# A four-layer graph network on one core: digraph mixes in float16 halves, delta turned by a transfer, norm statistics on ScalarE, the turned adjacency read from memory

## The reference, cut to what matters

```
x = layernorm(layer(x) + x)      # mean and variance over the 384 features, eps 1e-5
```

```
u = h @ h.T / sqrt(D); a = softmax(u); delta = a * adj
attn = delta / (sum(delta, -1) + 1e-10)
ctx = (attn * upper) @ (h @ wl.T + bl) + diag(attn) * (h @ ws.T + bs) + (attn * lower) @ (h @ wr.T + br)
h = relu((ctx - mean) / sqrt(var + 1e-12) * g + beta)
```

## Time and profile before

| | |
|---|---|
| median of 3 runs | 2745.75 us (2744.03 to 2746.03) |
| the profiled execution's own time | 2747.06 us |
| its span, first to last instruction | 2745.3 us |
| TensorE busy | 2590.6 us, 94% (granted clock 0.985 in the mean) |
| VectorE busy | 2315.3 us, 84% |
| GpSimd busy | 2123.3 us, 77% |
| ScalarE busy | 1758.2 us, 64% |

### The profile page before, as it was taken

The page is one execution under the profiler, slowest core; times in us unless marked ns, Lnnn a source line. Parts: engine busy times, 40 slices in busy tenths (PEclk is TensorE's granted clock), DMA queues, the critical chain, the costliest instruction groups (busy, mean ns, idle before and its releaser), DMA issues.

```text
span 2745.3 us, 90305 instructions
## 1 busy us (share of the span) xinstructions
PE 2590.6 (94%) x33792; PEld 1932.8 (70%) x33792; DVE 2315.3 (84%) x8232; ACT 1758.2 (64%) x4628; POOL 2123.3 (77%) x3211
## 2 busy tenths in 40 slices
PE   5899889999999999999999999999999999989996
PEld 4677667767677777777777777777776777667764
DVE  6789887879888888888888888888888888888877
ACT  6646666556666666666666666666666565666546
POOL 6577868777788788888788888888887777777675
PEclk9899999999999999999999999999999999999997
DMA  7733454344444544544545454454554453354315
GB/s 175 157 71 79 81 94 81 74 77 78 89 84 76 95 81 84 94 88 78 89 87 91 83 96 82 80 93 88 88 81 75 82 93 70 77 90 95 60 37 107
DMA packets 800731, 238.95 MB, mean 87 GB/s; under 512 B 767664, under 2 KB 799536, under 8 KB 800304
## 3 DMA queue, kind: packets, MB, share of 16 engines
q1 hardware_dynamic: 791840, 218.23, 44.8%
q10 hardware_dynamic: 8464, 14.94, 1.8%
HBM read 31.72 MB, written 12.58 MB: 16 GB/s over the span
## 4 chain that ended last, share of the span: by engine, by line
PE 54%; DVE 19%; POOL 11%; issue 5%; DMA 5%; ACT 4%; SPq 2%; DVEq 0%; POOLq 0%; ACTq 0%
PE bank L848 7%; PE bank L849 7%; PE bank L850 7%; PE bank L839 6%; PE bank L840 6%; PE bank L841 6%; DMA region<-region 3%; DVE region L1024 3%; PE bank L935 2%; PE bank L878 2%; PE bank L928 2%; PE bank L936 2%; POOL region L644 2%; POOL ab L671 2%; PE bank L864 1%
## 5 line engine op out<-in xcount | busy, mean ns | idle before, releaser
L839 PE MATMUL bank<-region,w_hi 128*128 128x128 f16 x3960 | 687.7, 220 | 7.4 <-DMA region<-region 2.6
L840 PE MATMUL bank<-region,w_hi 128*128 128x128 f16 x3960 | 686.6, 220 | 0.0
L841 PE MATMUL bank<-region,w_lo 128*128 128x128 f16 x3960 | 686.6, 220 | 0.0
L848 PE MATMUL bank<-w_hi,region 128*128 128x384 f16 x1815 | 596.5, 329 | 30.2 <-DMA region<-region 20.7
L849 PE MATMUL bank<-w_lo,region 128*128 128x384 f16 x1815 | 595.6, 328 | 0.0
L850 PE MATMUL bank<-w_hi,region 128*128 128x384 f16 x1815 | 595.6, 328 | 0.0
L655 POOL TENSOR_TENSOR region<-region 128x512 f16<-128x512 f32 x330 | 383.9, 1164 | 185.9 <-ACT region L776 184.1
L770 ACT ACTIVATE region<-region,small 128x128 f32<-128x128 f32 x1320 | 419.5, 392 | 79.3 <-DVE small L1030 61.1
L839 PEld LDWEIGHTS bank<-region,w_hi 128*128 128x128 f16 x3960 | 389.0, 98 | 32.5 <-issue 7.7
L840 PEld LDWEIGHTS bank<-region,w_hi 128*128 128x128 f16 x3960 | 388.8, 98 | 12.3 <-issue 5.8
L841 PEld LDWEIGHTS bank<-region,w_lo 128*128 128x128 f16 x3960 | 388.8, 98 | 0.0
(11 more groups left out here) (217 smaller groups left out, 7742.0 us busy)
## 6 DMA issues: line engine op xcount, KB each, us to landing
region<-region SPq DMA_TRANSPOSE x715, 3.1
last_unit<-w_dram ACTq DMA_DIRECT2D x19, 576.0 KB, 6.1
x<-x_dram SPq DMA_DIRECT2D x55, 192.0 KB, 2.6
out_dram<-region SPq DMA_DIRECT2D x55, 192.0 KB, 2.1
adj<-adj_dram SPq DMA_DIRECT2D x55, 64.0 KB, 2.3
rows<-rows_dram ACTq DMA_DIRECT2D x5, 576.0 KB, 4.4
last_unit<-last_unit SPq DMA_TRANSPOSE x117, 3.1
last_unit<-x_dram SPq DMA_DIRECT2D x9, 192.0 KB, 2.5
```

The lines of the kernel that those rows point to most:

```text
L839: pe.matmul(dst, lhsT=w_hi[:, w, k, cols], rhs=t_hi[u][:, k, :], start=(k == 0), stop=False)
L840: pe.matmul(dst, lhsT=w_hi[:, w, k, cols], rhs=t_lo[u][:, k, :], start=False, stop=False)
L841: last = pe.matmul(dst, lhsT=w_lo[:, w, k, cols], rhs=t_hi[u][:, k, :], start=False, stop=(k == DT - 1))
L848: pe.matmul(dst, lhsT=t_hi[u][:, k, :], rhs=w_hi[:, w, k, :], start=(k == 0), stop=False)
```

## The change

The mixes of the digraph layer become float16 products. `delta` is divided by its row sum and split into high and low (ScalarE, then VectorE), both turned by one transfer (128 x 256 float16), and masked by float16 triangles of 512 columns. Left and right product get their bias on VectorE, into the stage tile `z`, then a high part (ScalarE) and a low part (GpSimd); the right one's bias waits until the left one's low part has been read out of `z`. The self product keeps its way. The mix is six float16 products. The transposed adjacency is an input of its own and is loaded into `mask` by SP after the masked scores of layer 0. For the six norms over 384 features with a residual or in the digraph layer, the sum comes from the accumulator of the addition, and ScalarE makes the mean and the sum of squared distances. `PARTS`, `PERIOD` (22.0233) and `SHIFTED` (now one number per batch and stage for batches 0 to 15 and 50 to 63; before, one per batch for 0 to 11 and 50 to 63) are new; `plan()` is otherwise the same.

Core of the diff (declarations, signals, the tables of the planner and renamed constants are left out):

```diff
             def load_adj(i, k):
+                sp.wait_ge(*topped.at(i, HG - 1, DT - 1))
+                sp.dma_start(adj_t[i % UNITS], adj_t_d[i]).then_inc(adj_t_landed.of(i), 16)
...
+            def delta_turn(i, layer):
+                u = i % UNITS
+                sp.wait_ge(*mixed_out.at(i, "low delta", layer))
+                sp.dma_start_transpose(delta_t[u], delta_hl[u].rearrange("p a n -> p (a n)")).then_inc(landed.of(i), 16)
...
             def denominator(i, layer):
...
-                pool.tensor_scalar(col(u, EPS), col(u, DENOM), col(u, DENOM), 1e-12, ALU.mult, ALU.mult).then_inc(gpsimd_done.of(i), 1)
+                pool.tensor_tensor(col(u, INVERSE), col(u, DENOM), constant(MINUS_ONE), ALU.pow).then_inc(gpsimd_done.of(i), 1)
...
             def residual(i, layer):
-                pool.wait_ge(*numbers.at(i, "residual mv", layer))
-                pool.tensor_tensor(col(u, VAR), mv[u][:, 1:2], constant(LN_EPS), ALU.add).then_inc(gpsimd_done.of(i), 1)
+                pool.wait_ge(*scalar_done.at(i, "spread", layer))
+                pool.tensor_scalar(col(u, VAR), col(u, SQUARES), 1.0 / D, 1e-5, ALU.mult, ALU.add).then_inc(gpsimd_done.of(i), 1)
...
-                pool.tensor_scalar(col(u, SHIFT), mv[u][:, 0:1], col(u, ROOT), -1.0, ALU.mult, ALU.mult)\
-                    .then_inc(gpsimd_done.of(i), 1)
+                pool.tensor_tensor(col(u, SHIFT), col(u, MINUS_MEAN), col(u, ROOT), ALU.mult).then_inc(gpsimd_done.of(i), 1)
...
-            def turn_adj(i, k):
-                act.wait_ge(*multiplied.at(i, "adj"))
-                act.activation(adj_t[i % UNITS], bank("turn_adj", k, i)[:, 0:N], ACT.Copy).then_inc(scalar_done.of(i), 1)
...
+            def high_delta(i, layer):
+                act.wait_ge(*gpsimd_done.at(i, "row scale", layer))
+                act.activation(delta_hl[u][:, 0, :], delta[u], ACT.Copy, scale=col(u, INVERSE)).then_inc(scalar_done.of(i), 1)
+
+            def spread(i, layer):
+                act.wait_ge(*mixed_out.at(i, "added", layer))
+                act.activation(col(u, MINUS_MEAN), col(u, SUM), ACT.Copy, scale=-1.0 / D).then_inc(scalar_done.of(i), 1)
+                act.wait_ge(*scalar_done.at(i, "minus mean", layer))
+                act.activation(score_at[u], z[u], ACT.Square, bias=col(u, MINUS_MEAN), accum_out=col(u, SQUARES))\
+                   .then_inc(scalar_done.of(i), 1)
...
-                pe.transpose(bank("turn_delta", layer, i)[:, 0:N], delta[u], ident).then_inc(multiplied.of(i), 1)
...
             def mix(i, k):
-                    for w in L2_W[k - 2]:
-                        pe.wait_ge(*biased.at(i, "made", w))
+                    for w in (left, right):
+                        pe.wait_ge(*low_of_shifted.at(i, "made", w))
                     pe.wait_ge(*mixed_out.at(i, "delta3", k - 2))
-                    pe.matmul(made[:, 0:D], lhsT=triangles[u][:, 0, :], rhs=proj[u][0], start=True, stop=False)
-                    pe.matmul(made[:, 0:D], lhsT=triangles[u][:, 1, :], rhs=proj[u][2], start=False, stop=True)\
-                      .then_inc(multiplied.of(i), 1)
+                    for side, w in enumerate((left, right)):
+                        high, low = (triangles[u][:, side, n, :] for n in range(2))
+                        h = side_of(u, w)
+                        pe.matmul(dst, lhsT=high, rhs=h[:, 0, :], start=(side == 0), stop=False)
+                        pe.matmul(dst, lhsT=high, rhs=h[:, 1, :], start=False, stop=False)
+                        last = pe.matmul(dst, lhsT=low, rhs=h[:, 0, :], start=False, stop=(side == 1))
+                    last.then_inc(multiplied.of(i), 1)
...
             def add_bias(i, w):
+                    if w in SIDES[1::2]:
+                        dve.wait_ge(*low_of_shifted.at(i, "made", w - 2))
+                    scale, dst, src, bias = 1.0 / WSCALE, shifted[w][u], made[:, 0:D], rows[:, ROW_OF[w], :]
...
+            def delta_low(i, layer):
+                dve.wait_ge(*scalar_done.at(i, "high delta", layer))
+                dve.scalar_tensor_tensor(delta_hl[u][:, 1, :], delta[u], col(u, INVERSE), delta_hl[u][:, 0, :], ALU.mult, ALU.subtract)\
+                   .then_inc(mixed_out.of(i), 1)
...
             def turn_delta(i, layer):
-                dve.wait_ge(*multiplied.at(i, "delta", layer))
-                dve.tensor_tensor_reduce(out=score[u][:, 2, :], in0=turned, in1=ident, scale=1.0, scalar=0.0, op0=ALU.mult,
+                dve.tensor_tensor_reduce(out=score[u][:, 0, :], in0=delta[u], in1=ident, scale=col(u, INVERSE), scalar=0.0, op0=ALU.mult,
                                          op1=ALU.add, accum_out=col(u, DIAGONAL)).then_inc(numbers.of(i), 1)
-                dve.tensor_tensor(triangles[u], turned.unsqueeze(1).broadcast_to([128, 2, N]), tri[:, 0:2, :], ALU.mult)\
-                   .then_inc(mixed_out.of(i), 1)
+                dve.wait_ge(*landed.at(i, "delta", layer))
+                dve.wait_ge(*numbers.at(i, "diagonal", layer))
+                dve.tensor_tensor(triangles[u], delta_t[u].unsqueeze(1).broadcast_to([128, 2, 2, N]),
+                                  tri[:, :, :].unsqueeze(2).broadcast_to([128, 2, 2, N]), ALU.mult).then_inc(mixed_out.of(i), 1)
...
             def inner(i, k):
-                    dve.scalar_tensor_tensor(made[:, 0:D], proj[u][1], col(u, DIAGONAL), made[:, 0:D], ALU.mult, ALU.add)\
-                       .then_inc(numbers.of(i), 1)
-                    dve.wait_ge(*numbers.at(i, "summed", k))
+                    dve.scalar_tensor_tensor(made[:, 0:D], proj[u][1], col(u, DIAGONAL), made[:, 0:D], ALU.mult, ALU.add,
+                                             accum_out=col(u, SUM)).then_inc(numbers.of(i), 1)
+                    return
...
+            def centre(i, k):
+                dve.wait_ge(*scalar_done.at(i, "inner spread", k))
+                dve.scalar_tensor_tensor(inner_of(i, k), inner_of(i, k), col(u, MINUS_MEAN), rows[:, GAIN_ROW[k], :], ALU.add, ALU.mult)\
+                   .then_inc(numbers.of(i), 1)
...
             def residual(i, layer):
-                dve.wait_ge(*mixed_out.at(i, "added", layer))
-                dve.bn_stats(st6[u], z[u]).then_inc(numbers.of(i), 1)
-                dve.wait_ge(*numbers.at(i, "residual st", layer))
-                dve.bn_aggr(mv[u], st6[u]).then_inc(numbers.of(i), 1)
```

More of the change, by code:

```diff
@@ new lines @@
+    (SCALAR, "spread", 2): (-241.457, 0.830, 0.950, ((VECTOR, "residual", 2),), ()),
+    (VECTOR, "turn", 2): (-241.371, 0.465, 0.743, ((SCALAR, "turn", 2),), ()),
+    (PE, "mix", 2): (-240.152, 0.975, 1.150, ((VECTOR, "turn_delta", 0), (POOL, "low", 9), (POOL, "low", 11)), ()),
+    (POOL, "bias", 8): (-229.155, 0.955, 1.090, ((SCALAR, "project", 8),), ()),
+    (VECTOR, "residual", 2): (-215.835, 0.580, 0.750, ((VECTOR, "gain", 3),), ()),
+    (SCALAR, "u_gcn", 1): (-210.879, 0.200, 0.474, ((VECTOR, "u_gcn", 1),), ()),
@@ L1168 @@
         "adj_dram": _np.ascontiguousarray(a["adj"]),
+        "adj_t_dram": _np.ascontiguousarray(a["adj"].transpose(0, 2, 1)),
         "w_dram": _np.stack([_np.ascontiguousarray(w) for w in ws]),
```

542 lines of the change are left out of this document (292 added, 250 removed), and 30 rows, old and new, of the table SHIFTED.

## The result

The kernel after takes 2755.52 us (median of 7 runs, 2752.06 to 2765.58), the kernel before beside it 2746.03. The ratio is 1.0037, 95% interval 1.0022 to 1.0052: slower by 10 us, where 60 us of gain were forecast. The profiled execution took 2759.25 us, 3.7 above the median; its span is 2757.3. Each kernel has one profile, so a difference of under 4 us between two profiles may be chance.

What follows compares the result with a forecast made beforehand. TensorE, working 1186.40 of 1200 settled us, was taken as the bound. 2747 - 66 (TensorE) + 10 (idle growth) + 5 (longer drain) - 10 (new order) = 2686 us, 2685 for the median; range 2630 to 2742.

Steps and rivals of the forecast that it cites:

- what a batch costs on TensorE is paid 64 times: TensorE bounds the settled stretch, so its cost per batch counts in full for each of the 64 batches.
- paid part: TensorE's saving from float16 mixes and dropped turns: 1.04 us per batch, times 64 = 66 us (61 to 81).
- does not set the pace yet, and has over 30 us in hand: A batch's passage through its unit: 248.0 us for the first batch against 280 us that seven units give.
- Rival (d): The digraph mix gains nothing because its cost was something else: about 2730 us, chance 0.03.
- rival (b): VectorE's in-order queue waits for the turned delta's transfer, making the run slower: 2815 us at 2.0 us per wait, chance 0.09.
- my prices above hold as much: VectorE prices for two SBUF operands already include a mean excess of 0.25 us, as seen at L1124.
- Rival (e): Six new VectorE instructions with two SBUF operands each wait out a GpSimd one of 1.0 us: 2849 us, chance 0.02.
- Rival (a): Other engines eat the gain, TensorE starving with nobody full, 2.5% idle: about 2725 us or no change, chance 0.20.
- (c): Rival: the ends shrink, the new order giving back 50 of 141 us idle: about 2635 us, chance 0.14.
- -10: Term for the re-planned order of all queues, acting on idle time in the ends: middle of -50 to +30 us.

Runs made afterwards that it cites:

- a1: Kernel after with two products per digraph mix in place of six, low-part products left out: 2729.5 us, ratio 0.9944.
- a2: Kernel before with six float16 products of 384 columns in place of each digraph mix's two float32 ones: 2731.1 us, ratio 0.9950.
- e1: Kernel before with the four residual norms' VectorE statistics taken over 16 of 384 columns: 2727.6 us, ratio 0.9926.
- a3: Kernel after with ScalarE's six squares per batch over 16 columns in place of 384: 2755.5 us, ratio 1.0041.
- b1: Kernel after with the gain base and the sum of the masked u_gcn halves rewritten to one SBUF operand each, same results: 2728.5 us, ratio 0.9941.
- c1: b1 with the digraph's delta kept in its accumulator bank, which brings a new planned order: 2754.4 us, ratio 1.0034 against the kernel before.
- f3: Kernel before with its four residual norms' statistics moved to ScalarE, the old order kept: 2837.0 us, ratio 1.0343.
- f1: Kernel after with the product for the diagonal moved from just ahead of the triangles to just behind the low delta: 2745.3 us, ratio 1.0006.
- d2: c1 with the planner's wishes moved by a search and no instruction changed: 2726.1 us, ratio 0.9919 against the kernel before.

## Why the prediction was wrong

**What a TensorE microsecond is worth.** The step that failed first is "what a batch costs on TensorE is paid 64 times" and the 66 us "paid part". The trace does show 53 us less; a1 and a2 say that 0.3 of that comes out as time over the whole run, some 16 to 20 us. The reading behind it was wrong, 99% busy taken for a bound. TensorE's records last 0.33 us where the starts are 0.16 apart, so each can hide a wait of up to 0.17; e1 shows that VectorE counted in the kernel before too.

**The passage.** That the passage "does not set the pace yet, and has over 30 us in hand" set the 248.0 us of the first batch, which goes ahead of all others, against 280. In the settled stretch no unit stands free: its next load starts about 1 us after its last residual does. In the kernel before:

```profile
853.77 0.56 DVE L1131 SCALAR_TENSOR_TENSOR z<-bank,x 128x384 f32<-128x384 f32 x1 [1.28 <-PE bank L850]
854.88 0.58 SPq L594 DMA_DIRECT2D x<-x_dram  x1
```

and after:

```profile
876.08 0.56 DVE L1241 SCALAR_TENSOR_TENSOR z<-bank,x 128x384 f32<-128x384 f32 x1 [2.07 <-PE bank L950]
876.67 0.33 SPq L669 DMA_DIRECT2D x<-x_dram  x1
```

The first instruction on the new batch follows the landing by 1 to 2 us in the mean, so that a batch holds its unit for seven times 40.4 us, about 282, in both kernels. So the forecast's 30 us can't be seen there. How much of the 282 is waiting in queues, and whether an eighth unit would help, no run shows; a3 took 1.9 us of work out of it and gained nothing.

**Its sizes.** The mix was priced right: its six starts lie 0.16 apart, from L1028 at 1386.43 to the next group at 1387.40 it is 0.97 us, for 0.975 forecast. ScalarE's square was 0.615 for 0.62, the copy 0.196 for 0.20, the read 0.187; ScalarE 80% busy in the settled stretch for 86% forecast, VectorE 85% for 88%. Rival (d) is out. No table load came with Square: both profiles have one, of 1.28 us, at the start. The pace before was 40.4 us, not 40.0, and rival (b)'s sum, 2747 + 64 x 1.1, is 2817; neither moves the forecast.

**VectorE and its two-operand lines.** The triangles' 0.70 is right as a mean (0.688), and as a mean it hid that half of them take 0.97, the one at 1385.26 just ahead of its mix among them. The low delta was 0.549 for 0.38, the unchanged sum 0.616 for 0.380, the gain base 0.503 for 0.401. The sentence "my prices above hold as much" failed: the excess grew from about 0.7 to 2.4 us per batch. That VectorE's total came out as forecast, 1019.8 / 29.5 = 34.5 us per batch for 34.4, is luck: other items were cheaper, such as the residual of layer 0 (0.549 for 0.802). Rival (e) had the mechanism at 0.02 and priced it at a whole GpSimd instruction for each of six; the real excess was 0.07 to 0.35 for each of ten, and more of it on two unchanged lines than on the new ones. Those two alone are worth 26 us (b1), more than the 10 by which the change lost.

**Rival (b), the wait for the transfer.** Rejected: VectorE waited 0.2 and 1.1 us in 1200 for it. The Trainium skill ("VectorE: DVE Perf Modes", "The three transpose paths") has the DMA's turn cost more than TensorE's; no run here separates that cost.

**Rival (a)** named the right kind of thing, TensorE idle with nobody full, at 0.20 and too small: 36 us idle in the settled stretch for its 30, but 1 us of busy time was never worth 1. Of (c), nothing in sum: from 400 to 800 us the same 9.3 batches pass as before, and by the last residuals the kernel after comes to the 16th batch 22 us later and ends 15 us faster behind the 46th.

**The order.** "-10" stood for the re-planned queues, bounded by -50 and +30. Order alone moved b1 by +20, c1 by -32, and one exchange moved after by +39. With four of the statistics put into the old order the cost is +94. So the swings by order are as large as the term the forecast was built on, and -10 with these bounds was a guess. That the new plan is what kept the whole change at +10 is likely from f3 and a3, but the whole change was not run in the old order.

**What stays open.** At the measured worth of 0.3 for TensorE and 0.2 to 0.35 for VectorE, 53 and 39 us less work should give some 25 to 30 us; with the +10 the loss to be explained is 35 to 40. b1 accounts for 26 of it, roughly, as VectorE's 39 us are already net of the longer waits that b1 takes away. The remaining 10 or so lie in the longer way of delta and of the statistics or in the order; f1's 9 do not add to b1's, and no run here separates them. Delta turned by the transfer was not tried alone in the old kernel.

The quickest versions that compute the whole are b1 (0.9941) and d2 (0.9919), both quicker than both kernels; their intervals overlap.

## What to carry to other kernels

Before pricing a saving on the busiest engine at its full size, test its worth: shorten it a little in the kernel at hand, and look at how much comes out, by stretch; here it was a third over the run, with 99% busy, and between 0.3 and 0.7 in the middle by the order of the queues. In a kernel whose queues are written out, an instruction's duration at its place matters more than its mean, and a moved step must be judged together with a new order. Where GpSimd is busy and another engine waits behind it, give a small VectorE instruction one operand at most in SBUF: a one-column instruction cost 0.5 us for 0.15. Then time it: the same edit gave 26 us in one order and nothing in the other.

## What the runs showed of the hardware

- A VectorE instruction on one column with two SBUF operands took up to 0.942 us (1.110 in the kernel before), 0.151 at least; as a tensor_scalar with the second operand as its per-row scalar, 0.210 in the mean. The wait hits any length: 0.299 to 1.066 for the sum of 128 columns, 0.424 to 1.032 for the triangles.
- The wait ends with GpSimd's pass over 384 columns, and a fixed 0.01 to 0.28 us later the VectorE instruction ends. Behind GpSimd's power on one column (0.55 us) there is none, 48 times of 48.
- Removing one such wait moves it to the next: the low delta 0.549 to 0.628 in b1, L1233 0.549 to 1.325 in f1.
- VectorE masks 512 float16 columns from SBUF in 0.424 us when GpSimd lets it, what 256 float32 columns from a bank took the earlier trace rows.
- A statistics instruction over 16 columns takes 0.178 us, over 384 0.561; a ScalarE square 0.308 and 0.615.
